# Edge convolution with segment maximum: the set-up in another order, 60 early gathers, 29 picked steps

## The reference

```python
xn   = (x - mean(x, 0)) * rsqrt(var(x, 0) + 1e-5) * gamma + beta
feat = concat([xn[dst], xn[src] - xn[dst]], -1)        # 200000 x 128
h    = relu(feat @ W1 + b1)                            # W1 128 x 128
msg  = h @ W2 + b2                                     # W2 128 x 64
agg  = relu(where(isfinite(m := segment_max(msg, dst)), m, 0))
out  = layernorm(x + agg)                              # over the 64 features
```

## Time and profile before

| | us |
|---|---|
| median of 3 runs (2410.23 to 2418.83) | 2415.8 |
| the profiled execution | 2424.7 |
| its span | 2422.7 |
| PE / DVE / ACT / POOL busy | 1818.5 / 1292.7 / 862.0 / 1283.2 |

### The profile page before, as it was taken

How to read it: one execution, slowest core, us unless ns; L and a number is a source line. 1 busy time by engine, 2 the same in 40 slices (tenths; PEclk the granted TensorE clock), 3 DMA queues, 4 the chain that set the end, 5 groups by cost and what they waited for, 6 DMA issues and landing times.

```text
span 2422.7 us, 31826 instructions
## 1 busy us (share of the span) xinstructions
PE 1818.5 (75%) x12305; PEld 938.5 (39%) x12305; DVE 1292.7 (53%) x2070; ACT 862.0 (36%) x968; POOL 1283.2 (53%) x1356
## 2 busy tenths in 40 slices
PE   2046887787878778787878878878788778887785
PEld 1032444343434434343434444444444434444443
DVE  2054655565555555555555556556456555565553
ACT  2044443333333333333333333333334333333333
POOL 7715245556555565456555565555655565555621
PEclk6557899998999999898989899998999988898996
DMA  4154223233333332333323333233323333333320
GB/s 93 35 173 122 59 84 81 77 90 86 80 86 84 88 95 70 85 81 96 87 70 91 87 87 80 81 89 95 89 72 94 91 81 81 75 94 87 76 62 5
DMA packets 132832, 202.31 MB, mean 84 GB/s; under 512 B 74828, under 2 KB 76937, under 8 KB 132648
## 3 DMA queue, kind: packets, MB, share of 16 engines
q0 software_dynamic: 43440, 85.03, 16.5%
q1 hardware_dynamic: 87946, 115.04, 14.9%
q10 hardware_dynamic: 1294, 0.20, 0.1%
HBM read 189.19 MB, written 12.60 MB: 83 GB/s over the span
## 4 chain that ended last, share of the span: by engine, by line
another core or an unknown queue 38%; PE 29%; ACT 19%; issue 8%; DVE 5%; DMA 1%; SPq 0%; POOLq 0%; DVEq 0%; ACTq 0%
PE ps_g L1146 10%; PE ps_g L1153 6%; ACT hid L688 5%; ACT best L640 5%; PE ps_mr L1190 4%; ACT best L644 4%; ACT best L683 3%; PE ps_acc L1234 2%; DVE oh L919 2%; PE ps_h L1205 2%; PE ps_mr L1196 2%; PE ps_h L1215 1%; DVE runmax L993 1%; PE ps_h L1222 1%
## 5 line engine op out<-in xcount | busy, mean ns | idle before, releaser
L511 POOL DMA_INDIRECT xb<-b_dram,src_ix x1248 | 1181.1, 946 | 1031.4 <-PE ps_h L1205 384.9
L919 DVE TENSOR_SCALAR oh<-ps_k 128x1024 bf16<-128x1024 bf16 x1372 | 849.6, 678 | 1.0
L1146 PE MATMUL ps_g<-oh,xtab 128*128 128x512 bf16 x2744 | 643.5, 387 | 5.8 <-issue 5.0
L1190 PE MATMUL ps_mr<-hid,w 128*64 128x512 f32 x784 | 270.8, 776 | 369.9 <-ACT best L683 325.6
L972 DVE TENSOR_TENSOR best<-ps_acc,last_key 128x336 f32<-128x336 f32 x196 | 99.3, 507 | 815.8 <-remote 655.9
L683 ACT ACTIVATE best<-ps_mr 128x512 f32<-128x512 f32 x196 | 117.0, 597 | 1097.1 <-remote 816.3
L1146 PEld LDWEIGHTS ps_g<-oh,xtab 128*128 128x128 bf16 x2744 | 256.9, 99 | 375.6 <-issue 103.3
L1153 PE MATMUL ps_g<-oh,xtab 128*64 128x512 bf16 x2744 | 387.1, 424 | 12.6 <-issue 11.3
L993 DVE TENSOR_TENSOR_SCAN runmax<-rb,runmax,ps_mr 128x512 f32<-128x512 bf16 x196 | 249.6, 1274 | 97.4 <-PE ps_mr L1190 55.1
L688 ACT ACTIVATE hid<-ps_h,bias 128x1024 f32<-128x1024 f32 x196 | 217.9, 1112 | 106.8 <-remote 42.2
L1190 PEld LDWEIGHTS ps_mr<-hid,w 128*64 128x64 f32 x784 | 44.1, 154 | 479.6 <-ACT best L683 391.8
(11 more groups left out here) (181 smaller groups left out, 537.2 us busy)
## 6 DMA issues: line engine op xcount, KB each, us to landing
kb<-keys_dram SPq DMA_DIRECT2D x98, 504.0 KB
rb<-reset_dram SPq DMA_DIRECT2D x98, 256.0 KB
xb<-b_dram,src_ix POOLq DMA_INDIRECT x1248
src_t<-in_src SPq DMA_DIRECT2D x56, 256.0 KB
aw<-a_dram SPq DMA_DIRECT2D x196, 31.5 KB
a_dram<-oh SPq DMA_DIRECT2D x6, 672.0 KB, 3.5
xwin<-xp_dram SPq DMA_DIRECT2D x196, 10.5 KB
out<-y SPq DMA_DIRECT2D x182, 10.5 KB
```

The costliest lines, as they stand in the source:

```text
L511: pool.indirect_dma_start(xb[:, u, t, h, :], None, b_dram[:, :], bass.IndirectOffsetOnAxis(ap=src_ix[:, b, q + t, h:h + 1], axis=0))\
L919: dve.tensor_scalar(oh[0:PN, n % NOH, :], node_keys_ps, n % TN + 0.5, None, ALU.is_equal).then_inc(oh_ready, 1)
L1146: last = pe.matmul(ps_g[:, h, :], xtab[0:PN, t, 0:2, :].rearrange("p w c -> p (w c)"), oh[0:PN, n % NOH, h * GE:(h + 1) * GE], start=t == ...
L1190: last = pe.matmul(ps_mr[h * C:(h + 1) * C, :], w2[:, :], hid[:, j % 2, h, :], start=True, stop=True)
```

## The change

The constant `NFIRST = 8` is new: POOL gathers the rows of x for 8 steps (4 + 7 x 8 = 60 transfers) at the start, and those of the other four (32) only behind the branch, after all of table B is stored. Table B's staging takes four slots of `xb`, one area of table A and two slots of `kb`. SP stores table B behind the branch, after the first rows of table A and window 1, and loads windows 2 and 3 after it. ACT issues four transfers at the start instead of 13; gamma and beta follow the copies of x, the other three the squares. DVE computes edge keys and most of the flag before the mean, and the rest of the flag before it copies table B. TensorE makes table A unit by unit. Twelve instead of nine high parts of x (`x_hi_piece`) come after the keys. The node keys of the second picked segment move from step 1 to step 4. DVE waits in step 1 for all of table B. `PICKED` is 29. Cut to its core:

```diff
@@ -48,10 +48,11 @@
     AHEAD = 5
-    PICKED = 28
+    PICKED = 29
     REST = 8
     NX = 12
     NXB = 8
+    NFIRST = 8
     NS = 4
@@ -206,8 +207,9 @@
             .rearrange("p (s e) -> p s e", s=AS)
-        b_st = [xb[:, NX // 2 + g, :, :, :] for g in range(2)] + \
-            [a_slots[:, g, 0:TG * 2 * HID].rearrange("p (t h c) -> p t h c", t=TG, h=2) for g in (3, 0, 1, 2)] + [xb[:, NX // 2, :, :, :]]
+        b_st = [xb[:, u, :, :, :] for u in (NX // 2, NX // 2 + 1, NX // 2 - 2, NX // 2 - 1)] + \
+            [a_slots[:, AS - 1, 0:TG * 2 * HID].rearrange("p (t h c) -> p t h c", t=TG, h=2)] + \
+            [kb[:, u, :].bitcast(f32).rearrange("p (t h c) -> p t h c", t=TG, h=2) for u in (NS - 1, NS - 2)]
         pair = xs[:, 0, 0, :, :]
@@ -382,14 +384,6 @@
                     load_resets(0)
-            b_table = b_dram.rearrange("(p t) c -> p t c", t=TN)
-            for g in range(AG):
-                t0, t1 = 2 * g * TG, min(TN, 2 * g * TG + 2 * TG)
-                sp.wait_ge(b_even, g + 1)
-                sp.wait_ge(b_odd, min(g + 1, AU - AG))
-                for p0, p1 in ((0, 112), (112, PN)):
-                    sp.dma_start(b_table[p0:p1, t0:t1, :], b_st[g][p0:p1, :, :, :].rearrange("p t h c -> p (t h) c")[:, 0:t1 - t0, :])\
-                        .then_inc(b_first if g == 0 else b_out, 16)
             sp.wait_ge(flag_ready, 1)
@@ -432,7 +426,17 @@
                 load_table(0)
-                for w in range(1, NS):
+                load_window(1)
+                b_table = b_dram.rearrange("(p t) c -> p t c", t=TN)
+                for g in range(AG):
+                    t0, t1 = 2 * g * TG, min(TN, 2 * g * TG + 2 * TG)
+                    sp.wait_ge(b_even, g + 1)
+                    sp.wait_ge(b_odd, min(g + 1, AU - AG))
+                    for p0, p1 in ((0, 112), (112, PN)):
+                        sp.dma_start(b_table[p0:p1, t0:t1, :], b_st[g][p0:p1, :, :, :].rearrange("p t h c -> p (t h) c")[:, 0:t1 - t0, :])\
+                            .then_inc(b_out, 16)
+                sp.wait_ge(b_out, 32 * AG)
+                for w in range(2, NS):
                     load_window(w)
@@ -498,9 +500,6 @@
                 u = wide_slot(i)
-                if i == 0:
-                    pool.wait_ge(b_first, 32)
-                    pool.wait_ge(b_out, 32 * (AG - 1))
                 if i >= NXB:
@@ -513,12 +512,15 @@
             pool.wait_ge(src_ix_ready, 2)
-            for g in range(NX):
+            for g in range(NFIRST):
                 gather(g)
             pool.wait_ge(flag_ready, 1)
             windowed = pool.value_load(in_order[0:1, 0:1], min_val=0, max_val=1)
             with pool.If(windowed == 1):
                 pool.wait_ge(src_ix_ready, 5)
+                pool.wait_ge(b_out, 32 * AG)
+                for g in range(NFIRST, NX):
+                    gather(g)
                 for i in range(len(gathered) - NX):
@@ -550,19 +552,16 @@
         def _(act):
+            def twice(w, start, inner):
+                return bass.AP(tensor=w.tensor, offset=start, ap=[[0, 2], [inner, C], [1, inner]])
+
             act.wait_ge(pads_ready, 3)
             act.dma_start(first_a[:, 0, :], bass.AP(tensor=dst.tensor, offset=0, ap=[[0, 1], [WE, NW + 1], [1, 1]]),
                           allow_slow_non_contiguous=True).then_inc(win_in, 16)
             act.dma_start(first_a[:, 1, 0:NW], bass.AP(tensor=dst.tensor, offset=E - S, ap=[[0, 1], [WE, NW], [1, 1]]),
                           allow_slow_non_contiguous=True).then_inc(win_in, 16)
-            for h in range(2):
-                act.dma_start(w_b[h * C:(h + 1) * C, :], W1[C:2 * C, :]).then_inc(par_in, 16)
-                act.dma_start(gam[h * C:(h + 1) * C, :], gamma.rearrange("(c a) -> c a", a=1)).then_inc(par_in, 16)
-                act.dma_start(bet[h * C:(h + 1) * C, :], beta.rearrange("(c a) -> c a", a=1)).then_inc(par_in, 16)
-                act.dma_start(w_a[h * C:(h + 1) * C, :], W1[0:C, :]).then_inc(par_in, 16)
-            act.dma_start(w2[:, :], W2).then_inc(par_in, 16)
-            act.dma_start(b1c[:, :], b1.rearrange("(c a) -> c a", a=1)).then_inc(par_in, 16)
-            act.dma_start(b2b[:, :], b2.rearrange("(a c) -> a c", a=1).to_broadcast([P, C])).then_inc(par_in, 16)
+            act.dma_start(w_b[:, :], twice(W1, C * HID, HID)).then_inc(par_in, 16)
+            act.dma_start(w_a[:, :], twice(W1, 0, HID)).then_inc(par_in, 16)
             act.sem_inc(g_out, 16)
@@ -574,6 +573,8 @@
                     .then_inc(xt_sb, 1)
+            act.dma_start(gam[:, :], twice(gamma, 0, 1)).then_inc(par_in, 16)
+            act.dma_start(bet[:, :], twice(beta, 0, 1)).then_inc(par_in, 16)
             act.wait_ge(mean_ready, 1)
@@ -582,15 +583,17 @@
 
-            for g in range(4):
-                x_hi_piece(g)
+            act.dma_start(w2[:, :], W2).then_inc(late_in, 16)
+            act.dma_start(b1c[:, :], b1.rearrange("(c a) -> c a", a=1)).then_inc(late_in, 16)
+            act.dma_start(b2b[:, :], b2.rearrange("(a c) -> a c", a=1).to_broadcast([P, C])).then_inc(late_in, 16)
+            x_hi_piece(0)
             act.wait_ge(warm, 1)
             act.wait_ge(std_in, 1)
             act.activation(bn[:, 2:3], bn[:, 1:2], ACT.Sqrt).then_inc(std_ready, 1)
 
             def split_hi(u):
                 n = unit_tiles(u)
-                act.wait_ge(a_ps, u // 2 + 1)
+                act.wait_ge(a_ps, u + 1)
                 if u >= 2 * AS and u % 2 == 0:
@@ -613,10 +616,8 @@
                 act.wait_ge(b_ps, g + 1)
-                if g >= 2:
-                    act.wait_ge(a_out[(AG + g - 2) % AS], 32 * len(range((AG + g - 2) % AS, AG, AS)))
-                if g == AG - 1:
-                    act.wait_ge(b_first, 32)
+                if g == 4:
+                    act.wait_ge(a_out[AS - 1], 32)
                 act.activation(b_st[g][0:PN, 0:n, 0, :], ps_a[2 * (AG + g) % 4][0:PN, 0:n * HID].rearrange("p (t c) -> p t c", c=HID),
@@ -649,7 +650,7 @@
             node_keys(0)
-            for g in range(4, XG):
+            for g in range(1, XG):
                 x_hi_piece(g)
@@ -707,7 +708,7 @@
                         x_mid_piece(g)
-                    if segment < PICKED and k == first_step[segment - 1] + 1:
+                    if segment < PICKED and k == first_step[segment - 1] + (4 if segment == 1 else 1):
                         node_keys(segment)
@@ -784,6 +785,26 @@
+            dve.wait_ge(dst_in, 96)
+            chain(dve.tensor_scalar(win_key[:, :], dst_r[:, :, 1:2].rearrange("w h a -> w (h a)"), -1.0, None, ALU.add))
+            chain(dve.memset(win_key[0:1, 0:1], -1.0))
+            for h in range(2):
+                dve.tensor_scalar(keys[:, h, :], dst_r[:, h, 1:WE + 1], win_key[:, h:h + 1], None, ALU.subtract).then_inc(keys_ready, 1)
+            dve.tensor_tensor(step[:, :, :], dst_r[:, :, 1:WE + 2], dst_r[:, :, 0:WE + 1], ALU.subtract).then_inc(step_ready, 1)
+            dve.wait_ge(win_in, 32)
+            chain(dve.memset(first_a[:, 0, 0:1], 0))
+            chain(dve.tensor_copy(first_f[:, :, :], first_a[:, :, :]))
+            dve.sem_inc(firsts_ready, 1)
...
+            chain(dve.tensor_scalar(order[:, 4:5], first_f[:, 1, LB - 1:LB], -1.0, float(N - SL), ALU.mult, ALU.add))
             dve.wait_ge(xt_sb, AG)
@@ -800,15 +821,20 @@
-            dve.wait_ge(par_in, 176)
+            dve.wait_ge(par_in, 64)
...
+            dve.wait_ge(step_ready, 1)
+            dve.tensor_scalar(reset[:, :, :], step[:, :, 0:WE], SCALE, None, ALU.mult).then_inc(reset_ready, 1)
+            def take_src(n):
+                b0, b1 = SRC_GROUPS[n]
+                dve.wait_ge(src_ps, n + 2)
+                dve.tensor_copy(src_ix[:, b0:b1, :, :],
+                                ps_src[(n + 1) % 2][:, 0:(b1 - b0) * 2 * SB].rearrange("p (b h q) -> p b q h", h=2, q=SB))\
+                    .then_inc(src_ix_ready, 1)
+
+            dve.wait_ge(src_in, 32)
+            dve.tensor_copy(src_f[:, :, 1:NB, :], src_tv[0:SB, :, 1:NB, :]).then_inc(src_f_ready, 1)
@@ -832,51 +858,26 @@
             split_rest(0)
             for u in range(AU):
                 if u + 1 < AU:
                     split_rest(u + 1)
-                if u == 0:
-                    dve.wait_ge(src_in, 32)
-                    dve.tensor_copy(src_f[:, :, 1:NB, :], src_tv[0:SB, :, 1:NB, :]).then_inc(src_f_ready, 1)
                 split_lo(u)
-                if u in (3, 5, 7):
-                    take_src((u - 3) // 2)
-            for g in range(AU - AG):
-                dve.wait_ge(b_ps, g + 1)
-                if g >= 2:
-                    dve.wait_ge(a_out[(AG + g - 2) % AS], 32 * len(range((AG + g - 2) % AS, AG, AS)))
-                dve.tensor_copy(b_st[g][0:PN, 0:TG, 1, :], ps_a[(2 * (AG + g) + 1) % 4][0:PN, :].rearrange("p (t c) -> p t c", c=HID))\
-                    .then_inc(b_odd, 1)
-            dve.wait_ge(bias_ps, 1)
```

(59 more changed lines are left out.)

41 lines of the change are left out of this document (12 added, 29 removed).

## The result

The changed kernel took 2453.7 us (2453.35 to 2466.43, 6 runs); beside it the kernel before took 2419.66 (2410.23 to 2423.42, 6 runs). The ratio is 1.0148, interval 1.0125 to 1.0171: **1.5% slower**, where 0.5% faster was forecast, and above the range. The profiled execution took 2456.31 us, 31.6 more than that of before; its span is 2454.2.

The account below looks back on a forecast made before the run. Gather runs that delay TensorE's results were taken as the bound. 2424.7 - 18 (steps' lead) + 5 (29th pick) = 2411.7 profiled; from the runs' median, 2415.8 - 13 = 2403 us, 0.5% faster; 8-in-10 range 2373 to 2432.

Parts of the forecast that it names:

- Reading of the bound: Main loop and set-up: TensorE's results reach waiting engines only after POOL's gathers, about 1.7 us after the last one.
- Part 1 and 2: Set-up: 60 early gathers instead of 92, and reordered work, bring the first hidden layer to 132.3, 45.6 us earlier.
- Rival 3: Set-up: early hold not set by burst length, or TensorE held all through the 64-gather burst; +20 to +25, chance 0.2.
- signalling per unit: Table A in the set-up: signalling per unit instead of per pair costs nothing, bounds -5 to +3 us.
- Part 3: After the set-up: POOL restarts at 139, runs 64 gathers to 219; only the steps' lead is left, gain 18 us.
- two or three steps in the 70 us left: Inside the 64-gather run: that many steps advance, so step 4 or 5 stands at 221; gain 13 or 25 us.
- the 18 us: Price of one step inside a long gather burst, used to count the steps that advance during the 64 gathers.
- none advances, and the hold outlasts the burst: Lower bound for the lead of the steps after the set-up: 5 us slower.
- Part 4: Main loop: 29 picked steps with 49 extra selection tiles cost +5 us, bounds -4 to +18.
- The other 35 lie in burst steps: Main loop: of the 49 extra tiles, these 35 cost nothing, as TensorE is busy 8.46 of 11.72 us there.
- +10 for the dearer tiles: Main loop: sum for the 29th pick and its extra tiles beside picked steps, before +5 was taken for a higher clock.

Follow-up runs that it names:

- e14: Changed kernel with 28 picked steps, its first 12 gather groups behind the branch each tied to a hidden layer: 2377.86 us, ratio 0.9823 to the kernel before.
- e13: Changed kernel with 28 picked steps, on a chip with late results: 2431.97 us, ratio 1.0037 to the kernel before.
- e7: Kernel before with the 16 matmuls of its first pair of table units issued twice, on the chip without late results: 1718.23 us (one run).
- e12: Kernel before with 29 picked steps, on the chip without late results: 1753.65 us, ratio 1.0213 to the kernel before.
- e11: Repeat of e7 on the chip without late results (first table pair's 16 matmuls issued twice): ratio 1.0016 to the kernel before.
- e16: Kernel before with the first table pair's 16 matmuls issued twice, on a chip with late results: ratio 1.0016 to the kernel before.
- e3: Kernel before in its old order, with 60 gathers at the start and the other 32 behind the branch: 2441.57 us, ratio 1.0008 to the kernel before.
- e1: Kernel before with 29 picked steps and nothing else, on a chip with late results: 2463.33 us, ratio 1.0101 to the kernel before.
- e2: Changed kernel with 28 picked steps, on a chip with late results: 2447.11 us, ratio 1.0041 to the kernel before.
- e4: e2 with POOL waiting for a hidden layer before each of its first twelve groups behind the branch: 2398.78 us, ratio 0.9829 to the kernel before.
- e17: e15 with a lead over the hidden layers that grows by one with each picked step: 2366.48 us, ratio 0.9673 to the kernel before.
- e15: Changed kernel, 28 picked steps, 3 groups gathered early, every later group tied to a hidden layer: 2395.77 us, ratio 0.991 to the kernel before.

## Why the prediction was wrong, step by step

**Reading of the bound: right where results are late.** One observation of the kernel before ("whoever waits for it learns of it about 1.7 us after POOL's last gather") held in every trace with late results: behind the loop's runs of eight ACT's next copy of the maximum starts 1.8 to 1.9 us after the last gather (median of each trace). Breaking up POOL's run, and changing nothing else, gave 54 us (e14 against e13). I took it for a property of the kernel, however. It belongs to the kernel on some chips: the numbers on record for the chips with late results are 12, 2 and 6 (the chip of the first result has none on record), and 4 for the one without. Why they differ is open. By the Trainium skill, "SBUF — State Buffer" (SBUF: two separate sides), PE, ACT and VectorE's own pair never wait on anyone. The traces of e7 to e12 agree with that (in e11 ACT waits 2.79 us for the first table bank, in the middle of a run of gathers); the traces on the other chips don't (78.87 in e16). Whether it is the memory's port that holds the results there, no run shows.

**Part 1 and 2: right in the mechanism, 7.5 us short.** The early run ended at 82.2 (forecast 81.7), the chain resumed at 93.8 (94.1), the copies ended at 113.5 (121.1), the first hidden layer stood at 124.8 (132.3). Rival 3 with its early hold until 130 is out. The 7.5 us lie in table A: its last split was done 10.7 us behind the chain's restart (104.4), before 18.1 us behind it (134.82 to 152.87). That is the term of signalling per unit, "at nothing", and it lies outside my bounds of -5 to +3; how much of it is the signalling, no run shows. The gain vanished in the next step.

**Part 3: the failed step.** POOL restarted at 137.9 (139) and ran 64 gathers to 218.0 (219). The restart was hit by luck: the copies ended 7.6 us earlier than forecast, and from there it took 24.4 us, not 18.1. SP began its load 4.3 us behind them (I had 1), and 4.0 us passed between the end of its issues of table B and the gather at 137.92, for which I had nothing:

```profile
117.80 0.92 SPq L400 DMA_DIRECT2D aw<-a_dram  x2
...
130.36 3.60 SPq L436 DMA_DIRECT2D b_dram<-kb  x4
```

"I take two or three steps in the 70 us left" failed: none got through. I took the 18 us from step 0, and did not look at what was in it. In the trace of before TensorE has 26 matmuls in that step, which has no tile of selection (stretch and length, busy and count of TensorE, clock, DMA share, GB/s):

```profile
177.91:196.10 18.19, 7.25 (x26) 0.58 0.67 196
```

Step 2 is the first with selection: in the trace of before 64 matmuls lie between its hidden layer and the next (214.25 to 225.46), 28 of them for the first tiles. After, the stretch between these two layers with all engines:

```profile
145.92:229.28 83.36, 17.00 (x64) 6.19 (x66) 7.11 (x13) 4.88 (x8) 54.75 (x58) 0.56 0.26 76
```

82 us (146 to 228) for the 58 matmuls on record in between (48 up to the transposes of the maximum, 4 of x, 6 of the hidden layer) are 1.4 each; e16's table matmuls cost 2.3 each. The trace of before had such a figure: the 16 matmuls of the first pair of units had kept ACT waiting for 41 us, 2.6 each. At these prices no step with 64 of them fits into the 70 us left. So what failed is the price of 18 us a step: I had it from a step of 26 matmuls for steps of 64.

What the right price would have been is open, for there isn't one price per matmul. At the 0.7 us of step 0 (18.19 / 26) the 64 would have taken 45 us and fitted. Here are the same place in e13 (the hold was as long with 39 matmuls on record left) and the second to third hidden layer in e3 (56 matmuls, and inside a run of 64 a step did get through):

```profile
148.57:229.87 81.30, 17.57 (x39) 5.31 (x38) 5.97 (x11) 5.02 (x7) 52.99 (x56) 0.54 0.25 73
```

```profile
145.20:202.64 57.44, 17.02 (x56) 6.15 (x57) 7.37 (x14) 7.90 (x11) 43.42 (x47) 0.53 0.31 89
```

That is 2.1 and 1.0 us each. That the instructions count is shown for the table's first pair (e16); for a step it is argued.

So the set-up gave +5.6 instead of -18, just outside the bound of 5 us slower that I had named for this very case ("none advances, and the hold outlasts the burst"). It is also the second half of rival 3 ("if TensorE stays held all through the 64-gather burst"), whose price, +20 to +25, was too high.

**Part 4: mis-sized, +26.8 for +5.** "The other 35 lie in burst steps ... at nothing" held: 11.82 against 11.79. The price is in the picked steps, +1.37 us on average, of which the steps ahead of them give back 0.46. Taken in threes (the step ahead, the picked one, the one after), after has 5 beside runs of 16, at 37.8 us each, and 22 others at 33.8; before has 1 at 37.7 and 25 at 33.4. So some 17 of the 27 us go with four more runs of 16, and some 9 with the other threes, which got dearer by 0.4 each; three plain steps less for one three more give about 2 back, and 0.03 us on each plain step makes 3. The forecast's +10 for the dearer tiles was thus near, the merged runs were the term it lacked, and taking +5 in place of 10 was a guess at the clock, which stayed at 0.91. The trace of before had one warning, the 17.33 us step beside its run of 16, to which my forecast gave no price.

How firm is the link? Each run of 16 in the loops of before, after, e1, e13 and e16 has a picked step of 17.3 to 21.2 us beside it. The reverse does not hold: picked steps of 15.5 to 17.9 us stand without such a run in before, after, e1, e2, e4 and e14, and e17's run of 15 has a step beside it that is not picked (18.6). e17 against e15 shows that long picked steps and runs of 16 grow rare together when the waits change. Why the groups merge is argued only: the step ahead has few tiles and frees its slot at 9 us, before POOL is done with eight gathers (10 us). On a chip without late results the same edit costs 38 us another way, by TensorE's 0.655 us a tile. Nothing separates the two on a chip with late results, so how much of the +26.8 is plain TensorE work is open; the kernel with 29 picks and without merged runs wasn't tried.

**Sum.** 2424.7 + 5.6 + 26.8 - 0.9 = 2456.2. Of the 45 us between that and the forecast's 2411.7 the set-up is 24 (Part 3's price of a step inside the run) and the pick 22 (Part 4), less the 0.9.

## What to carry to other kernels

Where the trace shows TensorE's results late beside a run of gathers, do not take the time of one step inside a short run for that of another inside a long one: look how many TensorE instructions each has, and how long the run lasts. A few waits that break a run up can be worth more than the gathers' head start. Before picking a balance by a microsecond, look which engine is full: 49 tiles of 0.655 us are not free where that engine is TensorE.
